# Two convolution blocks on one core: the first two iterations of the deformable stage get an early load of y, two more hat slots and new orders

## What is computed

```python
out = relu(group_norm(conv(x, w1)))              # 1024 -> 256 channels
om = conv(out, w_off, pad=1) + b_off             # 27 channels: offsets and mask of 9 taps
mask = sigmoid(om[:, 2 * K:])
sampled = bilinear_sample(out, py, px) * mask    # at grid + offset, for each tap
out = relu(group_norm(einsum('bckhw,ock->bohw', sampled, w2)))
out = group_norm(conv(out, w3))                  # 256 -> 1024
return relu(out + x)
```

## Time and profile before

| | us |
|---|---|
| median of 3 runs | 2959.81 (2959.12 to 2959.93) |
| profiled execution | 2959.69 |
| its span in the trace | 2957.9 |
| around the span | 1.8 |

### The profile page before, as it was taken

One profiled execution on the slowest core, in us unless ns is written; L12 is line 12 of the kernel. 1 busy time (PEld: TensorE's weight loads), 2 busy tenths in 40 slices (PEclk: granted clock), 3 DMA queues, 4 the chain that ended last, 5 costly groups with the idle time before them and its releaser, 6 DMA issues.

```text
span 2957.9 us, 46557 instructions
## 1 busy us (share of the span) xinstructions
PE 2910.1 (98%) x16518; PEld 2869.1 (97%) x16518; DVE 2355.7 (80%) x5000; ACT 1796.4 (61%) x3281; POOL 252.8 (9%) x209
## 2 busy tenths in 40 slices
PE   9999999999998899999999999999999999999997
PEld 9999999999997899999999999999999999999997
DVE  5655889865666688888888888888888888888885
ACT  4544332346665466767667676676766767667664
POOL 0000000000000011111111111111111101111110
PEclk9999999999999899999999999999999999999998
DMA  7774111035653445444444444444445444444431
GB/s 270 216 238 133 44 44 44 10 121 218 248 229 130 123 135 156 152 151 158 150 158 152 149 158 149 159 150 150 158 147 163 147 149 158 149 158 152 150 118 74
DMA packets 209208, 437.39 MB, mean 148 GB/s; under 512 B 18640, under 2 KB 170192, under 8 KB 203344
## 3 DMA queue, kind: packets, MB, share of 16 engines
q1 hardware_dynamic: 159408, 326.82, 32.8%
q10 hardware_dynamic: 49568, 107.60, 11.8%
HBM read 307.71 MB, written 126.64 MB: 147 GB/s over the span
## 4 chain that ended last, share of the span: by engine, by line
PE 65%; DVE 2%; DMA 1%; ACT 1%; SPq 0%; issue 0%; POOL 0%; ACTq 0%; DVEq 0%; POOLq 0%
PE sample L87 7%; PE deform L87 7%; PE sample L88 7%; PE sample L92 7%; PE deform L92 7%; PE deform L88 7%; PE work L87 6%; PE work L92 6%; PE work L88 6%; PE work L74 1%; PE work L76 1%; PE work L75 1%; PE work L2051 1%; DMA hats<-hat_scratch 1%; PE sums_ps L1135 0%; PE work L2040 0%
## 5 line engine op out<-in xcount | busy, mean ns | idle before, releaser
L1465 ACT ACTIVATE v_hi<-sample 128x392 fp32r<-128x392 f32 (+1 forms) x640 | 292.1, 463 | 313.3 <-PE sample L92 304.5
L87 PE MATMUL sample<-s_hi,aT_hi 98*128 98x392 f32 (+1 forms) x1280 | 417.9, 332 | 8.2 <-DVE v_lo L1824 8.1
L88 PE MATMUL sample<-s_hi,aT_lo 98*128 98x392 f32 (+1 forms) x1280 | 414.2, 329 | 0.0
L87 PE MATMUL deform<-v_hi,w_w 128*128 128x392 f32 x1152 | 402.9, 350 | 0.0
L88 PE MATMUL deform<-v_hi,w_w 128*128 128x392 f32 x1152 | 392.6, 341 | 0.0
L1824 DVE TENSOR_TENSOR v_lo<-sample,v_hi 128x392 fp32r<-128x392 f32 (+1 forms) x640 | 327.1, 519 | 64.5 <-ACT v_hi L1465 63.0
L92 PE MATMUL sample<-s_lo,aT_hi 98*128 98x392 f32 (+1 forms) x1280 | 315.4, 327 | 0.0
L92 PE MATMUL deform<-v_lo,w_w 128*128 128x392 f32 x1152 | 310.4, 341 | 0.5 <-DVE v_lo L1824 0.4
L1456 ACT ACTIVATE s_hi<-hats 98x784 fp32r<-98x784 f32 x288 | 245.6, 853 | 100.2 <-DVE x L1712 71.9
L1816 DVE TENSOR_TENSOR s_lo<-hats,s_hi 98x784 fp32r<-98x784 f32 x288 | 278.8, 968 | 2.5 <-ACT s_hi L1456 1.6
L87 PEld LDWEIGHTS sample<-s_hi,aT_hi 98*128 98x128 f32 x1280 | 242.2, 189 | 11.6 <-issue 5.5
(11 more groups left out here) (226 smaller groups left out, 7308.9 us busy)
## 6 DMA issues: line engine op xcount, KB each, us to landing
hats<-hat_scratch SPq DMA_DIRECT2D x768, 150.1 KB
x<-in_x SPq DMA_DIRECT2D x64, 784.0 KB, 6.0
in_home<-y_scratch ACTq DMA_DIRECT2D x248, 196.0 KB, 3.1
out<-x ACTq DMA_DIRECT2D x62, 784.0 KB, 4.4
y_home<-in_x SPq DMA_DIRECT2D x32, 784.0 KB, 5.0
y_scratch<-y_out SPq DMA_DIRECT2D x16, 1568.0 KB, 5.9
terms<-in_x SPq DMA_DIRECT2D x30, 784.0 KB, 4.6
y_scratch<-y_home SPq DMA_DIRECT2D x15, 1568.0 KB, 5.1
```

The source lines that it names most:

```text
L87: nc.tensor.matmul(out, w_hi, x_hi, start=start, stop=False)
L88: nc.tensor.matmul(out, w_lo, x_hi, start=False, stop=False)
L1465: nc.scalar.activation(v_hi[:, group % 2, c, 0:taps_of(g), i, :], sample[:, t % 2, 0:cols(g)].rearrange("p (k s) -> p k s", s=PIX), ACT.Co ...
```

## The change

SP loads y of pair 1 in two halves of four tiles into `y_left`, each when pair 0's `add_y` has read that half. ScalarE's `load_y` starts with pair 2. Units 3 and 4 of pair 0 get a place of their own (`spare`) in the x1 buffer of pair 2; the load of pair 2's x waits until both are used. In place of the wait for their slot, these two loads wait until the unit with the same semaphore (unit 0, unit 1) has landed. ScalarE and VectorE get an order `first` for the iteration of pair 0; in it x1 of pair 1 is begun and the `w3` split comes before `part_om` and `add_taps`. `second` is rewritten, and TensorE does `group_a` of pair 1 after tile 3 and no longer after tile 6. Amount and kind of all arithmetic stay; eight DMAs of y become two. Indentation is cut by eight columns; empty lines are left out.

```diff
@@ -1285,6 +1285,16 @@
+spare = x1[0:HALF, 2].rearrange("p i k s -> p (i k s)")[:, 0:2 * 3 * 2 * PIX].rearrange(
+    "p (u e n) -> p u e n", u=2, e=3)
+def is_spare(p, u):
+    return p.n == 0 and u in (HATS, HATS + 1)
+def hat(p, u):
+    return spare[:, u - HATS] if is_spare(p, u) else hats[:, (UNITS * p.n + u) % HATS]
 def loads_until(p, u):
@@ -1298,16 +1308,27 @@
             sp.wait_ge(w3.lo_made, 1)
+        if p.n == 2:
+            sp.wait_ge(s_lo_made, HATS + 2)
         at_least(sp, out_stored[p.buf][i], 16 * p.lap)
...
                      x[p.n][:, i, :]).then_inc(x_loaded[p.buf][0], 16)
+    def load_second_y(half):
+        sp.wait_ge(plus_y, KX // 2 * (half + 1))
+        k = slice(KX // 2 * half, KX // 2 * (half + 1))
+        sp.dma_start(y_left[:, k].rearrange("p k i s -> p (k i s)"),
+                     y3[1][:, k, :].rearrange("p k s -> p (k s)")).then_inc(y_loaded[half], 16)
...
         slot, n = unit % HATS, 2 * PIX
-        at_least(sp, s_lo_made, unit - HATS + 1)
+        if is_spare(p, u):
+            sp.wait_ge(hats_loaded[slot], 48)
+        else:
+            at_least(sp, s_lo_made, unit - HATS + 1)
         if u < 2:
@@ -1324,10 +1345,10 @@
             src = hats_at[p.n % 2, 0, i, half * ROWS:(half + 1) * ROWS, t0:t0 + n]
-            sp.dma_start(hats[:, slot, half, 0:n], src.unsqueeze(1).broadcast_to([ROWS, SIDE, n])
+            sp.dma_start(hat(p, u)[:, half, 0:n], src.unsqueeze(1).broadcast_to([ROWS, SIDE, n])
                          ).then_inc(hats_loaded[slot], 16)
         src = hats_at[p.n % 2, 1, i, :, t0:t0 + n]
-        sp.dma_start(hats[:, slot, 2, 0:n], src.unsqueeze(0).broadcast_to([ROWS, SIDE, n])
+        sp.dma_start(hat(p, u)[:, 2, 0:n], src.unsqueeze(0).broadcast_to([ROWS, SIDE, n])
                      ).then_inc(hats_loaded[slot], 16)
@@ -1347,6 +1368,9 @@
         load_x(coming, 1)
+        if after is not None and after.n == 0:
+            load_second_y(0)
+            load_second_y(1)
         store_hats(after, 1, 0)
@@ -1374,7 +1398,7 @@
     def load_y(p, k):
-        if p.n == 0:
+        if p.n < 2:
             return
@@ -1383,10 +1407,13 @@
     @of_pair
-    def make_x1(p, k):
+    def whole_x1(p, k):
         act.wait_ge(plus_y, KX * p.n + k + 1)
...
                              bias=shift[:, k:k + 1]).then_inc(x1_made, 1)
+    @of_pair
+    def high_x1(p, k):
         act.wait_ge(x1_made, KX * p.n + k + 1)
@@ -1396,6 +1423,10 @@
+    def make_x1(p, k):
+        whole_x1(p, k)
+        high_x1(p, k)
     @of_pair
@@ -1453,7 +1484,7 @@
         at_least(act, sampled, tiles_until(unit - 2))
-        nc.scalar.activation(s_hi[:, unit % 2], hats[:, unit % HATS, 0:2],
+        nc.scalar.activation(s_hi[:, unit % 2], hat(p, u)[:, 0:2],
                              ACT.Copy).then_inc(s_hi_made, 1)
@@ -1523,44 +1554,51 @@
+    def first(after, coming):
+        for k in range(KX):
+            make_x1(after, k)
+        raw_a(after)
+        wo.make_hi(act, wo_stage, 1)
+        make_a(after, 0)
+        make_a(after, 1)
+        part_a(after)
+        w3.make_hi(act, w3_stage, 1)
+        for k in range(4):
+            whole_x1(coming, k)
+        part_om(after)
+        high_x1(coming, 0)
+        high_x1(coming, 1)
     def second(now, after, coming):
-        load_y(after, 1)
         make_distance(now, 0)
...
         make_mask(now)
-        load_y(after, 2)
-        make_x1(after, 0)
-        load_y(after, 3)
-        make_x1(after, 1)
+        high_x1(after, 2)
+        whole_x1(after, 4)
+        whole_x1(after, 5)
         part_aT(now, 0)
-        load_y(after, 4)
-        make_x1(after, 2)
-        load_y(after, 5)
-        make_x1(after, 3)
+        whole_x1(after, 6)
+        whole_x1(after, 7)
         part_aT(now, 1)
-        load_y(after, 6)
-        make_x1(after, 4)
-        load_y(after, 7)
-        make_x1(after, 5)
-        make_x1(after, 6)
-        make_x1(after, 7)
+        for k in range(RING, KX):
+            high_x1(after, k)
         part_s(now, 0)
         part_s(now, 1)
+        raw_a(after)
         part_v(now, 0)
...
         part_v(now, 3)
-        part_v(now, 4)
         part_s(now, 3)
-        part_v(now, 5)
-        raw_a(after)
-        part_s(now, 4)
-        part_v(now, 6)
         make_a(after, 0)
...
         part_a(after)
+        part_v(now, 4)
+        part_s(now, 4)
+        part_v(now, 5)
+        part_v(now, 6)
         part_s(now, 5)
@@ -1571,6 +1609,8 @@
     def step(past, before, now, after, coming):
+        if after is not None and after.n == 0:
+            return first(after, coming)
         if now is not None and now.n == 0:
@@ -1631,8 +1671,6 @@
         raw_a(after)
-        if after is not None and after.n == 0:
-            wo.make_hi(act, wo_stage, 1)
         write_y(before, 0)
@@ -1650,8 +1688,6 @@
         part_om(after)
-        if after is not None and after.n == 0:
-            w3.make_hi(act, w3_stage, 1)
         write_y(before, 6)
@@ -1707,8 +1743,11 @@
                 dve.wait_ge(x_loaded[p.buf][0], 32 * (p.lap + 1) - (16 if p.buf == 0 else 0))
-            dve.wait_ge(y_loaded[k % 2], 16 * (KX // 2 * (p.n - 1) + k // 2 + 1))
-        from_y = y_in[:, k % 2] if p.n else y_left[:, k]
+            if p.n == 1:
+                dve.wait_ge(y_loaded[k // (KX // 2)], 16)
+            else:
+                dve.wait_ge(y_loaded[k % 2], 16 * (KX // 2 * (p.n - 2) + k // 2 + 2))
+        from_y = y_in[:, k % 2] if p.n > 1 else y_left[:, k]
         nc.vector.scalar_tensor_tensor(x1[:, p.buf, :, k, :], from_y, scale[:, k:k + 1],
@@ -1806,14 +1845,14 @@
         dve.wait_ge(hats_loaded[slot], loads_until(p, u))
-        nc.vector.tensor_tensor(hats[:, slot, 0:2, 0:n], hats[:, slot, 0:2, 0:n],
-                                hats[:, slot, 2:3, 0:n].broadcast_to([HALF, 2, n]), ALU.mult).then_inc(s_made, 1)
+        nc.vector.tensor_tensor(hat(p, u)[:, 0:2, 0:n], hat(p, u)[:, 0:2, 0:n],
+                                hat(p, u)[:, 2:3, 0:n].broadcast_to([HALF, 2, n]), ALU.mult).then_inc(s_made, 1)
...
         dve.wait_ge(s_hi_made, unit + 1)
-        nc.vector.tensor_tensor(s_lo[:, unit % 2], hats[:, unit % HATS, 0:2],
+        nc.vector.tensor_tensor(s_lo[:, unit % 2], hat(p, u)[:, 0:2],
                                 s_hi[:, unit % 2].bitcast(F32), ALU.subtract).then_inc(s_lo_made, 1)
@@ -1842,43 +1881,63 @@
-    def second(now, after, coming):
-        rest_aT(now, 0)
+    def first(after, coming):
         add_y(after, 3)
         rest_x1(after, 1)
-        rest_aT(now, 1)
+        rest_x1(after, 2)
         add_y(after, 4)
-        rest_x1(after, 2)
+        rest_x1(after, 3)
         add_y(after, 5)
-        rest_x1(after, 3)
+        rest_x1(after, 4)
         add_y(after, 6)
-        rest_x1(after, 4)
+        rest_x1(after, 5)
         add_y(after, 7)
-        rest_x1(after, 5)
         rest_x1(after, 6)
         rest_x1(after, 7)
+        count_a(after)
+        moments(after, gn1, 0)
+        coefficients(after, gn1)
+        wo.make_lo(dve, wo_stage, 1)
+        add_y(coming, 0)
+        add_y(coming, 1)
+        rest_a(after)
+        add_y(coming, 2)
+        add_y(coming, 3)
+        w3.make_lo(dve, w3_stage, 1)
+        add_taps(after)
+        rest_om(after)
+        for k in range(4, KX):
+            add_y(coming, k)
+    def second(now, after, coming):
+        for k in range(RING):
+            rest_x1(after, k)
+        rest_aT(now, 0)
+        rest_aT(now, 1)
+        for k in range(RING, KX):
+            rest_x1(after, k)
         make_s(now, 0)
         make_s(now, 1)
-        make_s(now, 2)
         rest_s(now, 0)
         rest_s(now, 1)
-        make_s(now, 3)
+        make_s(now, 2)
+        count_a(after)
         rest_v(now, 0)
         rest_v(now, 1)
+        rest_s(now, 2)
+        moments(after, gn1, 0)
+        make_s(now, 3)
         rest_v(now, 2)
-        rest_s(now, 2)
+        rest_v(now, 3)
+        coefficients(after, gn1)
+        rest_s(now, 3)
         make_s(now, 4)
-        rest_v(now, 3)
         rest_v(now, 4)
-        rest_s(now, 3)
+        rest_a(after)
+        rest_v(now, 5)
+        rest_s(now, 4)
         make_s(now, 5)
-        count_a(after)
-        moments(after, gn1, 0)
-        rest_v(now, 5)
-        coefficients(after, gn1)
-        rest_s(now, 4)
         rest_v(now, 6)
-        rest_a(after)
         rest_s(now, 5)
@@ -1902,9 +1961,10 @@
     def step(past, before, now, after, coming):
+        if after is not None and after.n == 0:
+            return first(after, coming)
         if now is not None and now.n == 0:
             return second(now, after, coming)
-        fresh = None if after is not None and after.n == 0 else after
         rest_v(before, 16)
@@ -1949,8 +2009,6 @@
         coefficients(after, gn1)
-        if after is not None and after.n == 0:
-            wo.make_lo(dve, wo_stage, 1)
         rest_s(now, 4)
@@ -1965,8 +2023,6 @@
         rest_om(after)
-        if after is not None and after.n == 0:
```

(8 more changed lines are left out.)

## The result

| | before | after |
|---|---|---|
| median of 7 runs, us | 2959.65 (2958.08 to 2961.06) | 2949.31 (2945.46 to 2951.74) |
| ratio, 95% interval | | 0.9963 (0.9952 to 0.9975) |
| span of the profiled execution | 2957.9 | 2947.7 |

The change makes the kernel 10.3 us faster by the medians, 10.2 us in the profiled spans. 12.7 were forecast. The runs of the changed kernel lie 6 us apart (lowest to highest), those of before 3.

What follows compares the result with a forecast made beforehand. TensorE, busy 98% of 2957.9 us, bounds the kernel; 22.5 us were lost between 947.20 and 1001.34. 22.5 - 10.4 + 0.8 = 12.9, step by step 12.6, taken as 12.7: 2947.0 us, range 2941.5 to 2954.

Steps and rivals of the forecast that it cites:

- The sum: Between first conv1 of pair 1 and third spread, 10.4 us lost in place of 22.5, start 0.8 earlier: 12.7 taken.
- y in two halves: Both halves of pair 1's y there by some 927 us; conv1 takes 8.6 us, ending at 955.0.
- First iteration: Pair 0's iteration: w3 split moved, two high_x1 instead; first conv1 of pair 1 0.8 us earlier, at 946.4.
- Hats: Third DMA of a unit lands 4.08 us after issue, 5.71 at most; units 3 and 4 at about 960 and 962.3.
- VectorE's order: TensorE's waits in sampling of pair 0 under VectorE's new order, 8.6 us in all; offsets start at 979.3.
- The slow clock: In sampling of pair 0 the clock falls once; tiles 2 and 3 at half speed cost 1.8 us more.
- The rival in which the clock stays up: TensorE's shorter, scattered waits in sampling leave its clock up: 16 us gained, 2943.7 us; chance 0.17.
- Given back later: Behind 1020 us, where VectorE is 86% busy, some 9 us are given back: 2956 us, no change; chance 0.07.
- hats late: All units land 1.6 us later, or a second slow stretch comes: 8 us gained, 2951.7 us; chance 0.14.
- clock down: TensorE at half speed from first conv1 to tile 12: end 8.3 us later, 2968 us; chance 0.02.

Runs made afterwards that it cites:

- the second timing: The changed kernel once more, with no edit, beside other kernels on the same chip: 2946.69 us, ratio 0.9959.
- the filled kernel: The changed kernel with 9 unread matmuls ahead of sample tile 0 of pair 0 and 13 behind tile 1: 2943.27 us, ratio 0.9946.
- count_a late: The changed kernel with VectorE's rest_v(0) and rest_v(1) ahead of count_a, without unread matmuls: 2945.21 us, ratio 0.9956.
- the four kernels with filling: The changed kernel with 22 unread matmuls: alone 2943.27 us; without hat places 2944.91; with count_a behind rest_v(1) 2942.17; that with rest_v(2) before product 3 2942.40.

## Why the prediction was right, and where it was off

**The sum.** 12.7 us forecast, 10.3 measured and 12.2 in the second timing (2958.94 - 2946.69). The range, the sign and the cause hold: these were TensorE's waits in two iterations, TensorE is full behind them, and the gain stays. With the terms as measured below, the same sum is 22.5 - 5.9 - 7.2 + 1.8 = 11.2 us: 5.4 us too little for the slow clock, 2.7 too much for the waits and 1.0 too little for the start. That the number came so near is in part luck, since the error in the waits goes the other way than the one in the clock. (A slip beside it: 0.89 and a third of 0.07 make 0.91 for faster, not 0.92.)

**y in two halves.** Right to 0.2 us: no wait of VectorE for y, none of TensorE for x_lo, conv1 in 8.78 us.

**First iteration.** The start of conv1 was forecast 0.8 us earlier and is 1.8 from the mark. The w3 split was priced right as to its own steps: 1.89 us away, and two high_x1 that take 0.93 together; the mask starts 0.66 us earlier (9.83 against 10.49 from the mark), not the whole difference of 0.96, since ScalarE now waits 0.29 us for the spread ahead of the distances. The term was too small in what follows. From the mask to aT_hi four x1 instructions stood, now three: 0.7 us more. Before, the first aT_lo stood behind an add_y that waited 0.78 us for its y, and conv1 waited 0.28 us for aT_lo: without that, 0.4 us more. Early y alone, with the old orders, brought 0.5. The w3 split put back costs 1.4 us at conv1, and more behind it, as hats hang on the distances too.

**Hats.** The bounds of 4.08 and 5.71 us hold, and only the third unit was far from the lower one that I took: unit 0 landed within 4.1 us of the issue of its third DMA (its product at 952.88 does not wait), unit 1 in 4.5, and unit 2 in 5.36. The chain that ended last has the link:

```profile
953.35 5.36 DMA hats<-hat_scratch
```

Of the two prices for a landing, the row is the nearer. The estimate of 2.3 us, worked out from the Trainium skill (DMA: Bandwidth & Descriptors, Anatomy of one DMA), is too low by 2.2 us for unit 1 and by 3.0 for unit 2; that section gives its fit for DMAs issued by GpSimd, and SP issues these. The part on units 3 and 4 failed in what it implied: their landing at 960 and 962 was listed as if it were part of the gain, where the new order asks for unit 3 only at 967. Without the places the medians show no loss. The working had both numbers and did not set one against the other.

**VectorE's order.** Forecast waits 1.6, 2.85, 1.6, 0.95, 0.5 and 1.1, 8.6 in all; measured 1.67, 2.40, 0.49, 0.21, 0.29 and 0.86, 5.9 in all. Place and releaser of the first two were right, and that count_a makes the second is shown by its run. The third is short because TensorE came to it late: in the filled kernel, with the clock up, it is 1.18. The next three were forecast too long whatever the clock, as they are 0.27, 0.30 and 0.85 in the filled kernel too.

**The slow clock.** This is the step that failed: "tiles 2 and 3 at half speed cost 1.8 us more". It was sized as before, where tiles 2 and 3 ran slowly and the clock was back at 974.7, 3.6 us after the wait of 4.73 had ended. Here the stretch lasted until 972.1: two tiles, group_a, the first deform part and nearly two more tiles ran in it, all at 1.2 GHz, and a second, short one came at 989, where none was forecast. From conv1 to the third spread 44.7 us passed for work that takes 31.6 at full clock; less 5.9 of waits this leaves 7.2 us, for the slow clock and some short gaps, where 1.8 stood. The forecast also called 960 to 970 the idlest stretch of before, but by the earlier trace rows that is 950 to 960, with TensorE busy for 5.22 us at a clock of 0.88; it fell at 957.7, behind waits of 1.26 and 2.75 us, and at 968, inside the one of 4.73. Filling the first two waits took the long stretch away and brought 3.4 us. The rival in which the clock stays up was thus wrong for this kernel, and its price fits another: it gave 3.3 us more than the forecast, and filling brought 3.4 by the second median.

**Given back later, hats late, clock down.** None of them: from 992.6 to about 2860 us TensorE is full at 2.4 GHz but for one wait of 0.9 us, and the 0.7 us by which the forecast erred behind the offsets lie where the second slow stretch begins.

## What to carry to other kernels

Where an engine near 100% has one gap, follow what ends it in order, and price each link with the others gone: here y alone gave 2.8 us, two hat places alone 5.1, both 8.8, and with new orders the places brought nothing that the medians show, so test each part again when all are in. A resource that was the longest link (a slot, a buffer) can be replaced by asking for its content later. After the waits of TensorE are cut, what the remaining ones do to its clock can cost more than they last (7.2 us against 5.9 here), and unread matmuls into an unused bank brought 3 us of it back. Where the medians of one kernel lie as far apart as the effects that are sought, a distance between two rows of the profile tells them better apart.

## What the runs showed of the hardware

- The slow stretch outlasts its cause. After 4.1 us of waits (1.67 and 2.40, within 955.8 to 962.1) TensorE worked at 1.2 GHz until 972.1, and of the 10 us from 962.1 it was busy in all but about 0.5. The clock came back 3.6 us after the last long wait in the kernel before (971.15 to 974.7), 6.7 us after it with count_a late (958.06 to 964.8), 10 us in the changed kernel and 12 in its second profile (960.68 to 972.8). The Trainium skill (TensorE: Matmul & The Clock Gate, "What's actually happening") says that the clock is halved by idleness and given back by activity; the trace agrees in kind. Why the way back took so different a time is open: in the last two a pause of 0.49 us lies on it, in the others none.
- Two executions of one program differ in the number and place of such stretches: in the first profile of the changed kernel the short one at 989.2 to 992.6 is there, in the second the clock is 1.00 from 980 to 1000; of the four kernels with filling two have one at 985 to 989 and two have none. The spans of the two profiles of the changed kernel differ by 5.4 us, but by 0.2 from the mark to the third spread. The rest is 1.1 us ahead of the mark, 0.8 behind the third spread by the short stretch, 1.9 between 1025 and 2829 us, where the first profile has one wait of 0.9 us more, and 1.5 at the end, where the clock of the first is 0.68 from 2875 to 2880 and that of the second 1.00.
- A hat unit's last DMA of 150 KB landed 4.1 to 5.7 us after its issue began in the chain of before, and 5.4 us after it in the chain of after, with the DMA engines 45% busy in 950 to 960.
